# A graph layer stack on one core: the attention sum's first two groups of edges are fetched one stage earlier

## The reference

```
q, k, v = (xn @ Wq.T + bq, xn @ Wk.T + bk, xn @ Wv.T + bv)          # 8 heads of 32
score = einsum('ehd,ehd->eh', q[edge_dst], k[edge_src])             # clipped to -10..10
ex    = exp(score - smax[edge_dst])
wv    = segment_sum(ex / den[edge_dst] * v[edge_src], edge_dst)     # then @ Wp.T + bp
mix   = ball_mixer(xn)       # convolution, batch norm over all nodes, linear attention, output projection
x     = x + gnn(xn) + mix
```

## Time and profile before

| | us |
|---|---|
| three runs | 3318.79, 3336.0, 3340.76 |
| median | 3336.0 |
| profiled execution, its own time | 3329.39 |
| its span, first to last instruction | 3327.7 |
| TensorE busy (share of the span) | 2521.4 (76%) |
| VectorE busy | 2118.3 (64%) |
| ScalarE busy | 1258.2 (38%) |
| GpSimd busy | 1263.6 (38%) |

### The profile page before, as it was taken

The page is one execution under the profiler, slowest core; times in us unless marked ns, Lnnn a source line. Parts: engine busy times, 40 slices in busy tenths (PEclk is TensorE's granted clock), DMA queues, the critical chain, the costliest instruction groups (busy, mean ns, idle before and its releaser), DMA issues. The chain is left out here.

```text
span 3327.7 us, 62976 instructions
## 1 busy us (share of the span) xinstructions
PE 2521.4 (76%) x17412; PEld 2029.6 (61%) x17412; DVE 2118.3 (64%) x4254; ACT 1258.2 (38%) x2585; POOL 1263.6 (38%) x971
## 2 busy tenths in 40 slices
PE   5547655677659999867677777777756966999997
PEld 5435443666547777643466666656545855899986
DVE  7655455654458888855558887788956556444455
ACT  1432210411145555433344545445334342454441
POOL 0058775688600000000566666666642001111125
PEclk9668855799859999978789999998976977999998
DMA  5337675233200000015666555656552004566633
GB/s 137 95 81 210 167 183 139 69 81 83 66 20 10 19 9 19 19 47 164 162 166 156 157 155 148 166 145 167 151 152 71 0 17 156 168 237 234 222 123 89
DMA packets 251663, 387.61 MB, mean 116 GB/s; under 512 B 117456, under 2 KB 175661, under 8 KB 246878
## 3 DMA queue, kind: packets, MB, share of 16 engines
q0 software_dynamic: 151392, 170.67, 20.7%
q1 hardware_dynamic: 87224, 202.62, 19.1%
q10 hardware_dynamic: 12864, 12.06, 1.3%
HBM read 323.76 MB, written 60.56 MB: 115 GB/s over the span
## 5 line engine op out<-in xcount | busy, mean ns | idle before, releaser
L922 POOL DMA_INDIRECT ms_got<-gather,edge_src x400 | 525.4, 1313 | 172.2 <-issue 118.3
L2128 POOL DMA_INDIRECT xz_rows<-gather_kv,edge_src x205 | 280.4, 1368 | 151.4 <-PE ab_total L2304 96.2
L2128 POOL DMA_INDIRECT ab_gkv<-gather_kv,edge_src x200 | 274.0, 1370 | 150.0 <-PE ab_total L2304 88.7
L970 PE MATMUL ms_total<-ms_got,ms_hot 125*125 125x256 f16 x1040 | 182.0, 342 | 179.1 <-DVE ms_hot L943 133.9
L970 PEld LDWEIGHTS ms_total<-ms_got,ms_hot 125*125 x1040 | 155.8, 176 | 212.6 <-issue 212.1
L1636 ACT ACTIVATE ex_h<-ex_up,ex_now 128x313 f32<-128x313 f32 (+1 forms) x320 | 195.9, 612 | 198.1 <-PE ex_up L701 190.9
L3051 DVE CAST moe_hidden<-moe_h 128x256 f16<-128x256 f32 (+1 forms) x336 | 100.7, 300 | 204.4 <-ACT moe_h L2988 202.4
L1852 POOL MEMSET br_one<- 125x1 f16 x1 | 0.1, 106 | 604.7 <-POOLq L126 604.7
L2988 ACT ACTIVATE moe_h<-moe_up,wring 128x256 f32<-128x256 f32 (+1 forms) x336 | 162.6, 486 | 129.3 <-PE moe_up L701 66.5
L2287 PE MATMUL ab_picked<-y_rows,xz_rows 125*125 x1060 | 161.6, 308 | 43.4 <-issue 35.3
L2287 PEld LDWEIGHTS ab_picked<-y_rows,xz_rows 125*125 x1060 | 135.6, 152 | 73.7 <-issue 71.5
(11 more groups left out here) (527 smaller groups left out, 5879.2 us busy)
## 6 DMA issues: line engine op xcount, KB each, us to landing
wring<-wsplit SPq DMA_DIRECT2D x33, 2052.0 KB
ab_dsts<-in_dst SPq DMA_DIRECT2D x83, 305.2 KB
wsplit<-mix_split SPq DMA_DIRECT2D x32, 512.0 KB
mix_raw<-in_L_ffn_W1p SPq DMA_DIRECT2D x16, 512.0 KB
mix_raw<-in_L_ffn_W2p SPq DMA_DIRECT2D x16, 512.0 KB
results<-moe_made SPq DMA_DIRECT2D x32, 256.0 KB, 7.5
ms_got<-gather,edge_src POOLq DMA_INDIRECT x400
gather_kv<-qkv_out SPq DMA_DIRECT2D x5, 1120.0 KB
```

Of the source, the lines that this page charges most:

```text
L922: pool.indirect_dma_start(out=self.got[:, s, j, :], out_offset=None, in_=self.m.gather0, in_offset=bass.IndirectOffsetOnAxis(ap=self.m.edg ...
L970: ins = pe.matmul(self.total[:, visit % 2, 0:C], self.hot[:, visit % RING, j, :], self.got[:, s, j, p * C:(p + 1) * C], start=(j + p == 0) ...
L2128: pool.indirect_dma_start(out=gkv[s][:, j, 0:2 * C], out_offset=None, in_=m.gather_kv, in_offset=bass.IndirectOffsetOnAxis(ap=m.edge_src[: ...
```

## The change

A new class `FirstGroups` holds the gather buffers, the node buffers, three small constants and their semaphores, in memory that lives over both stages. In `ball_rows` GpSimd now makes the constants and gathers groups 0 and 1 behind its mask. SyncE loads the nodes of groups 0 and 1 behind the copies of x and z and ahead of the five stores. VectorE waits for the copies (with a semaphore of their own now, `moved`) and zeroes `summed` there, behind the means and ahead of the four weighings. TensorE's 24 matmuls of the means move behind the products of the moments. `attention_and_ball` starts its gathers at group 2 and its node loads at group 2; VectorE zeroes only the banks. Groups 0 and 1 use the buffers with their own memory, groups 2 and 3 those over z.

```diff
+class FirstGroups:
+    GATHERED = 4
+    W = C + X8
+
+    def __init__(self, m, ph, dst):
...
+        self.own = ph.sb("gkv", [R, 2, J, C + self.W])
+        self.gkv = [self.own[:, s, :, :] for s in range(2)]
+        at = T * self.W
+        for s in range(self.GATHERED - 2):
+            self.gkv.append(m.xz_flat[:, at:at + J * (C + self.W)].rearrange("p (j w) -> p j w", j=J))
+            at += J * (C + self.W)
...
+    def number(self, pool):
+        pool.iota(self.node[:, :], ...).then_inc(self.s_node, 1)
+        pool.iota(self.minus_node[:, :], ...).then_inc(self.s_node, 1)
+        pool.memset(self.zeros[:, :], 0.0).then_inc(self.s_node, 1)
+
+    def gather(self, pool, g):
+        s = g % self.GATHERED
+        for j in range(J):
+            pool.indirect_dma_start(
+                out=self.gkv[s][:, j, 0:2 * C], out_offset=None, in_=self.m.gather_kv,
+                in_offset=bass.IndirectOffsetOnAxis(ap=self.m.edge_src[:, g, j:j + 1], axis=0)
+            ).then_inc(self.s_got[s], 16)
+
+    def load(self, sp, g):
+        e = g % G * (J * R)
+        sp.dma_start(self.dsts[:, g % 2, :], self.dst[e:e + J * R].unsqueeze(0).broadcast_to([R, J * R]))\
+            .then_inc(self.s_dst[g % 2], 16)
@@ ball_rows, GpSimd, behind the mask
+                early.number(pool)
+                for g in range(2):
+                    early.gather(pool, g)
@@ ball_rows, SyncE
-                    sp.dma_start(m.kept_x[part, :, :], m.x[part, :, :]).then_inc(s_kept, 16)
-                    sp.dma_start(m.kept_z[part, :, :], m.z[part, :, :]).then_inc(s_kept, 16)
+                    sp.dma_start(m.kept_x[part, :, :], m.x[part, :, :]).then_inc(s_moved, 16)
+                    sp.dma_start(m.kept_z[part, :, :], m.z[part, :, :]).then_inc(s_moved, 16)
+                for g in range(2):
+                    early.load(sp, g)
                 for c in range(CHUNKS):
...
-                sp.wait_ge(s_kept, 16 * (4 + CHUNKS))
+                sp.wait_ge(s_kept, 16 * CHUNKS)
+                sp.wait_ge(s_moved, 64)
@@ ball_rows, TensorE
-                for o in range(OB):
-                    for b in range(CB):
-                        ins = pe.matmul(turned_means[:, o:o + 1], wc[...], mean[:, b:b + 1], ...)
                 for q in range(CB):
...
                         ins.then_inc(s_mm, 1)
+                for o in range(OB):
+                    for b in range(CB):
+                        ins = pe.matmul(turned_means[:, o:o + 1], wc[...], mean[:, b:b + 1], ...)
                 pe.wait_ge(s_weighed, 2 * CB)
@@ ball_rows, VectorE
                 dve.tensor_scalar(mean[:, :], bank[:, 1, 0:CB], 1.0 / N, None, ALU.mult).then_inc(s_means, 1)
+                dve.wait_ge(s_moved, 64)
+                dve.memset(m.xz_flat[:, 0:T * early.W], 0.0)
                 for q in range(CB):
@@ attention_and_ball, GpSimd
-                pool.iota(node[:, :], ...)
-                pool.iota(minus_node[:, :], ...)
-                pool.memset(zeros[:, :], 0.0).then_inc(s_node, 1)
-                for g in range(G + 1):
+                for g in range(2, G + 1):
...
+                    early.gather(pool, g)
@@ attention_and_ball, SyncE
                 rows(0)
-                for g in range(2):
-                    load(g)
                 for g in range(2, GP):
                     sp.wait_ge(s_dfree, g - 1)
@@ attention_and_ball, VectorE
-                dve.memset(summed, 0.0).then_inc(s_zero, 1)
                 dve.memset(total[:, :, :], 0.0).then_inc(s_zero, 1)
-                dve.wait_ge(s_zero, 2)
+                dve.wait_ge(s_zero, 1)
```

More of the change, by code:

```diff
@@ L1812, in __init__, with ball_rows @@
         self.shift = ph.sb("shift", [128, OB])
-def ball_rows(nc, m, a, ball):
+class FirstGroups:
+    GATHERED = 4
+    W = C + X8
+    def __init__(self, m, ph, dst):
+        self.m, self.dst = m, dst
+        self.node = ph.sb("node", [R, T])
+        self.minus_node = ph.sb("minus_node", [R, T])
+        self.zeros = ph.sb("zeros", [R, R], F16)
+        self.dsts = ph.sb("dsts", [R, 2, J * R], I32)
+        self.own = ph.sb("gkv", [R, 2, J, C + self.W])
[4 more added lines that the diff above has]
+            at += J * (C + self.W)
+        self.behind = at
+        self.s_node = ph.sem("node")
+        self.s_got = [ph.sem(f"got{s}") for s in range(self.GATHERED)]
+        self.s_dst = [ph.sem(f"dst{s}") for s in range(2)]
+    def number(self, pool):
+        pool.iota(self.node[:, :], pattern=[[R, T]], base=0, channel_multiplier=0,
+                  allow_small_or_imprecise_dtypes=True).then_inc(self.s_node, 1)
+        pool.iota(self.minus_node[:, :], pattern=[[-R, T]], base=0, channel_multiplier=-1,
+                  allow_small_or_imprecise_dtypes=True).then_inc(self.s_node, 1)
+        pool.memset(self.zeros[:, :], 0.0).then_inc(self.s_node, 1)
[10 more added lines that the diff above has]
+            .then_inc(self.s_dst[g % 2], 16)
+def ball_rows(nc, m, a, ball, early):
     with phase(nc, "br") as ph:
@@ L1845, in ball_rows @@
             ph.sem(x) for x in ("row", "mean", "means", "moments", "mm", "weighed", "var", "sd"))
-        s_kept = ph.sem("kept")
+        s_kept, s_moved = ph.sem("kept"), ph.sem("moved")
         col = m.col
@@ L2034, in _, with attention_and_ball @@
                 v.link(dve.tensor_scalar(ball.scale[:, :], ball.scale[:, :], 1.0 / WS, None, ALU.mult))
-def attention_and_ball(nc, m, dst, ball):
+def attention_and_ball(nc, m, ball, early):
     import math
@@ L2055, in attention_and_ball @@
     UNITS = len(PARTS) * OB + 4 * J
-    GATHERED = 4
+    GATHERED = early.GATHERED
     PICKS = 3
@@ L2060, in attention_and_ball @@
     with phase(nc, "ab") as ph:
-        W = C + X8
+        W = early.W
         summed = m.xz_flat[:, 0:T * W].rearrange("p (t w) -> p t w", t=T)
-        at = T * W
-        gkv = []
-        for s in range(2):
-            gkv.append(m.xz_flat[:, at:at + J * (C + W)].rearrange("p (j w) -> p j w", j=J))
-            at += J * (C + W)
-        pick = m.xz_flat[:, at:2 * T * C].bitcast(F16)[:, 0:PICKS * J * R].rearrange("p (k n) -> p k n", k=PICKS)
-        more = ph.sb("gkv", [R, GATHERED - 2, J, C + W])
-        gkv += [more[:, s, :, :] for s in range(GATHERED - 2)]
+        gkv, dsts, node, minus_node, zeros = early.gkv, early.dsts, early.node, early.minus_node, early.zeros
+        s_node, s_got, s_dst = early.s_node, early.s_got, early.s_dst
+        pick = m.xz_flat[:, early.behind:2 * T * C].bitcast(F16)[:, 0:PICKS * J * R].rearrange("p (k n) -> p k n", k=PICKS)
         q16 = m.q16
-        dsts = ph.sb("dsts", [R, 2, J * R], I32)
-        minus_node = ph.sb("minus_node", [R, T])
-        node = ph.sb("node", [R, T])
         apart = ph.sb("apart", [R, J * R], BF16)
-        zeros = ph.sb("zeros", [R, R], F16)
         score = ph.sb("score", [R, J * X8])
@@ L2097, in attention_and_ball @@
         o_bank = ph.ps("o_bank", [128, 512])
-        s_node, s_zero = ph.sem("node"), ph.sem("zero")
-        s_got = [ph.sem(f"got{s}") for s in range(GATHERED)]
-        s_dst, s_dfree = [ph.sem(f"dst{s}") for s in range(2)], ph.sem("dfree")
+        s_zero, s_dfree = ph.sem("zero"), ph.sem("dfree")
         s_apart, s_pick, s_pickv, s_picked, s_qk = (ph.sem(x) for x in ("apart", "pick", "pickv", "picked", "qk"))
@@ L2126, in _ @@
                         pool.sem_inc(s_pace, 1)
-                    for j in range(J):
-                        pool.indirect_dma_start(
-                            out=gkv[s][:, j, 0:2 * C], out_offset=None, in_=m.gather_kv,
-                            in_offset=bass.IndirectOffsetOnAxis(ap=m.edge_src[:, g, j:j + 1], axis=0)
-                        ).then_inc(s_got[s], 16)
+                    early.gather(pool, g)
             @block.sync
             def _(sp):
-                def load(g):
-                    e = g % G * (J * R)
-                    sp.dma_start(dsts[:, g % 2, :], dst[e:e + J * R].unsqueeze(0).broadcast_to([R, J * R]))\
-                        .then_inc(s_dst[g % 2], 16)
                 def rows(c):
@@ L3207, in graph_layers @@
             ball = BallWeights(ph)
-            ball_rows(nc, m, a, ball)
-            attention_and_ball(nc, m, a["dst"], ball)
+            early = FirstGroups(m, ph, a["dst"])
+            ball_rows(nc, m, a, ball, early)
+            attention_and_ball(nc, m, ball, early)
         attention_out(nc, m)
```

15 lines of the change are left out of this document (5 added, 10 removed).

## The result

Six runs of the changed kernel have a median of 3301.61 us (3298.25 to 3312.55), six of the kernel before in the same measurement 3327.32 (3316.95 to 3340.76). The ratio is 0.993, with a 95% interval of 0.9909 to 0.9951: 16 to 30 us faster. A second measurement of the same kernel gave 0.9944 (0.9926 to 0.9963), about 18 us. The sum of the prediction was 16.0 us, 0.48%, and a time within 1% of the one before.

What follows compares the result with a forecast made beforehand. The attention sum's first 32 us were taken as a pipeline being filled, waiting for gathers and nodes. -19.1 + 1.5 + 2.0 - 0.4 = -16.0 us, from the 3336.0 median to 3320 us; range 3303 to 3337.

Steps and rivals of the forecast that it cites:

- The start, -19.1: Attention sum's start: with first gathers, nodes and memset moved out, group 1's multiply comes 19.1 us earlier.
- Late waits, +1.5: Attention sum's start: new waits for group 2's gather (0 to 1.9 us) and nodes (0 to 3.9) cost 1.5 us.
- Weights, +2.0: Ball rows' start: early gathers share the DMA engines with the weight loads, delaying the stage by 2.0 us.
- Rival (b): Ball rows' start: weights finish behind the gathers, +22 us, net +4, 3340 us; chance 5%.
- The copies, nothing: Ball rows: copies of x and z end 6.7 to 13.3 us later, still before the memset wants them; no cost.
- The end, -0.4: Ball rows' end: the memset is free with 3.2 us to spare, and TensorE's reordering gains 0.4 us.
- Rival (c): Attention sum: the first ball chunk lands late for its convolution, taking 13.9 us back, 3334 us; chance 5%.
- rival (d): Attention loop: later gathers may stall VectorE at single groups, so the gain is not kept; 3310 to 3334 us; chance 8%.

Runs made afterwards that it cites:

- nodesonly: Kernel before with only the node loads of groups 0 and 1 and the small constants moved early; ratio 0.9987 (0.9971 to 1.0004).
- allfour: Changed kernel that also gathers groups 2 and 3 in the ball rows' stage, once z is read and copied; ratio 0.9932 to the kernel before.
- nogather: Changed kernel with the ten gathers of groups 0 and 1 put back into the attention stage; 3311.85 us, ratio 0.9978 to the kernel before.
- after_again: The changed kernel measured once more without any edit; 3302.31 us against 3320.72 for the kernel before, ratio 0.9944.
- copieslate: Changed kernel with the copies of x and z, and node loads behind them, held until the first product from the weights; one execution, 3289.07 us.
- splitbefore: Kernel before with each node load cut into 112 and 13 rows, nothing moved; 3298.68 us against 3317.27, ratio 0.993.
- zeroonly: Changed kernel with constants, gathers and node loads put back; only the memset and TensorE's new order stay early; ratio 0.9989 to the kernel before.

## Why the prediction was right, step by step

**The start, -19.1: right in mechanism and size.** multiply(0) stands 6.73 us behind the stage's start (7.16 by the prediction's working), multiply(1) leads by 19.3, multiply(2) by 19.5. Its parts were tried singly, at multiply(1): the memset alone gives 0.7, gathers and nodes alone 13.6, both 19.3. What the working missed is inside it: it took the nodes for something that is merely waited for, while their loads slow the gathers (nodesonly: 7 us at multiply(1)). The sum did not suffer, since both were moved.

**Late waits, +1.5: nearly absent.** In the first profile of the change nobody waited for the nodes or the gather of group 2. In the second VectorE waited 0.94 us for the gather and ScalarE 1.33 us for the nodes (the two rows below). allfour, which takes the gathers of groups 2 and 3 off the stage, moved no offset up to multiply(6) by more than 0.3.

```profile
1597.93 1.49 DVE L2404 TENSOR_TENSOR ab_qk<-ab_picked,xz_rows 125x1280 f32<-125x1280 f32 x1 [0.94 <-DMA xz_rows<-gather_kv,edge_src]
```

```profile
1590.86 0.82 ACT L2203 ACTIVATE ab_apart<-bx_dsts,bx_minus_node 125x625 bf16<-125x625 int32 x1 [1.33 <-DMA bx_dsts<-in_dst]
```

The step that failed is the queue's speed: I let group 2 land where group 0 had, 20.4 us into the stage, but group 0 had shared the engines with two node loads. Group 2 landed by 18.0 and at 18.8 us, about where group 0 does once those loads are gone (18.5 in nogather). Instead of shrinking, the lead grew, to 21.8 and 23.0 us at multiply(6). That TensorE's picks ran at a higher granted clock (0.79 against 0.55 over the stretch) fits it; no run separates the two.

**Weights, +2.0: not there.** In seven of eight profiles with early gathers they came after 6.83 to 7.73 us, against 7.41 to 8.02 in the five without. Once, in after_again, they came after 10.34, 2.5 late, as the term had it:

```profile
1520.89 1.49 ACT L1933 ACTIVATE bx_w<-br_wc 128x1536 f16<-128x1536 f32 x1 [7.83 <-DMA bx_wr<-turned_res]
```

Rival (b), weights behind the gathers, is out. The step that failed is the overlap. The working had the gathers' bytes on the engines from the end of the first issue, 2.7 us after the stage's start. By the traces' packets the first of them began only 6.5 to 6.8 us after it (5.3 in copieslate), though the first issue began at 1.56 us; and the weights' last packet ended after 6.5 to 7.3 us (six profiles). Before that end the gathers had moved 0.01 MB at most; in copieslate it was 0.08 MB, in after_again 0.10 MB, there with the last weights coming in among packets of the copies. In the attention stage the first packet began 1.8 us behind the start of the first issue in the kernel before and 4.5 in splitbefore, here 5.0; why, no run shows. So what gathers cost weights that they really run beside was not measured.

Behind the weights, the rows show that the copies of x and z take nearly all the bytes: 4.81 MB against 0.25. The Trainium skill (DMA: Bandwidth & Descriptors, Queues, rings and completion order) says that an engine serves its queues in turn, a packet each. The near-equal counts, 208 and 233, with 20 times the bytes agree with it, if the packets that the profile counts are the section's, which no row shows. The prediction shared bytes by demand and never asked for the size of a packet.

**The copies, nothing: right, by a wrong reading.** The prediction took the copies for done near 1537, because the DMA share falls to 0.40 there; their last packet ended at 1545.5, 29.5 us into the stage. With early gathers it ended after 32.4 to 34.7 us (37.6 in copieslate), so 3 to 5 us later and not 7 to 13. The memset at 50.5 us found them done.

**The end, -0.4: right.** The memset was nearly free, with 0.9 us to spare in the first profile instead of 3.2, because the products and the narrow matmuls that cover it took 9.5 us and not 11.6; that it began 1.2 us behind the products was made up by the quicker weighings. In zeroonly and allfour, where the products were faster still, TensorE waited 0.67 us for the weighings behind it. The reordering gives 0.6 to 1.9.

**The sum.** In the two profiles of the change the attention stage is 10.5 and 23.4 us shorter, 17.0 in the mean (17.6 predicted for it), the ball rows 1.4 shorter and 0.4 longer (1.6 longer predicted). The timed medians say 25.7 (6 runs against 6; 23 by the ratio) and 18.4 (6 against 25). That is the term for the start, 19.1, with next to nothing taken off: of the two costs that I set against it, 3.5 us together, little was there. Of the second interval, 12 to 25 us, 16.0 and 19.5 are both inside, so the timed runs alone would not have shown this. Rival (c), the late ball chunk, did not show (L701 without a wait); rival (d) is what the first profile looked like, and after_again showed most of it to be that execution's.

## What to carry to other kernels

Price a moved transfer twice, for who waits for it and for what it slows while it runs; here a small load that did not look like what ended last was worth as much, once cut in two, as the whole move (0.993 each). Before moving work out of a start-up, list what ends last there and second to last: at the first multiplies the memset was worth 0 alone and 6 us behind the gathers. When queues share the engines, compare the sizes of their packets, not only their bytes. And before charging one transfer for another, look when its first packet really starts, not when it was issued.

## What the runs showed of the hardware

- Two broadcast loads of 125 rows of 2500 bytes, each issued as one DMA, delayed gathers on another queue by 3 us (first group) and 7 us (second). With every such load cut into 112 and 13 rows, the kernel took 0.993 (0.9909 to 0.9951) of its time. In the first 31 us of the stage the gathers then got 63.6% of the engines' time and 4.35 MB, against 58.7% and 4.10 MB. The Trainium skill (DMA: Bandwidth & Descriptors, Why a DMA increments its semaphore by 16 and not by 1) says that such a DMA runs on as many engines as the largest divisor up to 16 of its outer size: 5 for 125, 16 for 112, 13 for 13. The gain agrees with that, and so do the packets, at most 7 at once before (for the longest time 5) and up to 17 once split; no trace here names the engine of a packet.
- Copies of the rows x and z from the chip to DRAM moved in packets of 25,600 bytes, and left the gathers' queue, with packets of 4096 and 8 bytes, 5% of the engines' time.
- From the issue of the first gather to its first packet it took 1.8 us in the attention stage of the kernel before, 4.5 us in that of splitbefore, and 5.0 us in the changed kernel's ball rows, beside the loads and copies of SyncE's queue.
- A 5.56 us memset on VectorE beside the gathers cost them nothing at multiply(0) (21.2 us with it, 21.3 without) and at most 0.7 us at multiply(1) (31.9 and 31.2).
